# Attention's scan on TensorE: stationary operands of 64 tokens, two in the array, in place of halves of 32 tokens

## The reference, cut to what matters

```
scores  = einsum('bcihn,bcjhn->bcijh', Cc, Bc) * Lm * dtc      # inside a chunk, causal
y_intra = einsum('bcijh,bcjhp->bcihp', scores, xc)
y_cross = einsum('bcthn,bchnp,bcth->bcthp', Cc, h_states, exp(dAcs))
y = y_intra + y_cross + xp * D_param
```

## Time and profile before

| | |
|---|---|
| Time, median of 3 runs | 2917.99 us (2916.21 to 2919.55) |
| Profiled execution, its own time | 2926.86 us |
| Its span | 2925.1 us |
| TensorE matmul, busy | 2769.8 us, 95% of the span |
| TensorE weight load, busy | 2237.4 us, 76% |
| VectorE, busy | 2053.4 us, 70% |
| ScalarE, busy | 1715.0 us, 59% |
| GpSimd, busy | 1463.4 us, 50% |
| Mean granted clock | 0.988 |
| Scan matmuls (L1105) | 16384 records, 169.3 us busy |

### The profile page before, as it was taken

The page is one execution under the profiler, slowest core; times in us unless marked ns, Lnnn a source line. Parts: engine busy times, 40 slices in busy tenths (PEclk is TensorE's granted clock), DMA queues, the critical chain, the costliest instruction groups (busy, mean ns, idle before and its releaser), DMA issues.

```text
span 2925.1 us, 135112 instructions
## 1 busy us (share of the span) xinstructions
PE 2769.8 (95%) x59836; PEld 2237.4 (76%) x59836; DVE 2053.4 (70%) x2871; ACT 1715.0 (59%) x3424; POOL 1463.4 (50%) x2319
## 2 busy tenths in 40 slices
PE   8999999999999999999999999999677787899998
PEld 7888888888888888888888888887566676455554
DVE  6777777777777777777777777777444443788998
ACT  5666566566666666656656656665333333666674
POOL 4666666666667667666666666666110000111111
PEclk9999999999999999999999999999899998899999
DMA  4222222222222222222222222222644443578776
GB/s 154 78 73 69 74 78 76 73 78 77 72 79 74 72 82 73 73 77 74 75 75 78 74 72 79 76 73 58 215 132 136 110 123 119 178 222 269 234 228 195
DMA packets 262711, 316.37 MB, mean 108 GB/s; under 512 B 28000, under 2 KB 184032, under 8 KB 260464
## 3 DMA queue, kind: packets, MB, share of 16 engines
q1 hardware_dynamic: 252176, 297.55, 33.7%
q10 hardware_dynamic: 9952, 10.17, 1.1%
HBM read 194.31 MB, written 113.31 MB: 105 GB/s over the span
## 4 chain that ended last, share of the span: by engine, by line
PE 89%; DVE 4%; issue 4%; DMA 1%; SPq 1%; POOL 1%; ACT 0%; ACTq 0%; DVEq 0%; POOLq 0%
PE a_proj L991 41%; PE a_mix L991 12%; PE s_ps L1714 6%; PE g_pick_ps L1465 6%; PE a_scan L1105 5%; PE s_ps L1735 4%; DVE g_picked L1394 3%; PE s_ps L1730 3%; PE a_scan L1082 3%; PE a_scan L1069 2%; PE g_acc_ps L1489 2%; PE a_mix L1057 2%; PE a_misc L1049 1%; PE a_misc L1123 1%; DMA part_dram<-res 1%
## 5 line engine op out<-in xcount | busy, mean ns | idle before, releaser
L991 PE MATMUL a_proj<-wdh,xTh 128*128 128x512 f32 x1024 | 421.2, 411 | 5.5 <-issue 3.7
L991 PE MATMUL a_proj<-wdh,xTl 128*128 128x512 f32 x1024 | 402.4, 393 | 0.3 <-issue 0.3
L991 PE MATMUL a_proj<-wdl,xTh 128*128 128x512 f32 x1024 | 400.0, 391 | 1.7 <-issue 1.7
L823 DVE COPY_PREDICATED scan_in<-mask,a_scan 64x512 f32<-64x512 uint32 x512 | 382.4, 747 | 16.1
L1671 ACT COPY s_stage<-s_ps 128x1024 f32<-128x1024 f32 x256 | 279.2, 1147 | 150.9 <-PE s_ps L1714 142.4
L464 POOL TENSOR_TENSOR dx<-xs,d_row 64x512 f32<-64x512 f32 x256 | 331.4, 1294 | 15.1
L472 POOL TENSOR_TENSOR yv<-yt,dx 128x512 f32<-128x512 f32 x128 | 189.0, 1476 | 293.2 <-DVE yt L863 293.2
L639 ACT ACTIVATE scan_in<-CT,hsel 64x128 f32<-64x128 f32 x1024 | 326.2, 388 | 4.8
L603 ACT ACTIVATE raw<-a_proj,rs 128x272 f32<-128x272 f32 x128 | 62.5, 488 | 427.4 <-PE a_proj L991 427.4
L1394 DVE COPY g_picked<-g_pick_ps 128x1024 f32<-128x1024 f32 x128 | 156.7, 1224 | 218.4 <-PE g_pick_ps L1465 218.4
L1691 DVE STREAM_TRANSPOSE s_turned<-s_stage 128x2048 f32<-128x2048 f32 x128 | 294.4, 2302 | 9.8 <-ACT s_stage L1671 9.8
(11 more groups left out here) (152 smaller groups left out, 7275.3 us busy)
## 6 DMA issues: line engine op xcount, KB each, us to landing
x<-in_x_dram SPq DMA_DIRECT2D x128, 256.0 KB, 2.7
xn_dram<-xn SPq DMA_DIRECT2D x128, 256.0 KB, 2.4
part_dram<-res SPq DMA_DIRECT2D x128, 256.0 KB, 2.5
g_xn<-xn_dram SPq DMA_DIRECT2D x512, 64.0 KB, 2.3
s_part<-part_dram SPq DMA_DIRECT2D x128, 256.0 KB, 4.1
out_dram<-s_out SPq DMA_DIRECT2D x128, 256.0 KB, 3.8
xr<-in_xT_dram SPq DMA_DIRECT2D x126, 256.0 KB, 2.9
s_inner<-inner_dram SPq DMA_DIRECT2D x32, 512.0 KB, 4.1
```

Of the source, the lines that this page charges most:

```text
L823: nc.vector.copy_predicated(dst, mask[rows_, :].unsqueeze(1).unsqueeze(1).to_broadcast([CH, 4, 2, CH]), src).then_inc(mt_cp, 1)
L991: last = nc.tensor.matmul(out, lhs[a], rhs[c], start=(k == 0 and n == 0), stop=(k == nk - 1 and n == 2))
```

## The change

For each head and chunk the loop over two halves of 32 tokens is gone. The stationary operand is the whole slice of 64 tokens, and the output goes to 64 PSUM partitions at once: chunk 0 uses the array's columns 0 to 63, chunk 1 columns 64 to 127. Per scan there are 32 program matmuls where there were 64. The moving operand, the contraction over 128 rows, the outputs, all semaphores and all other functions are the same.

```diff
             for h in range(H):
                 for c in range(2):
-                    for i in range(0, CH, 32):
-                        out = scan_bank[CH * c + i:CH * c + i + 32, 2 + h // 8, HALF + h % 8 * HD:HALF + (h % 8 + 1) * HD]
-                        last = nc.tensor.matmul(out, scan_in[c][:, h, i:i + 32], xs[c][n % 4][:, h, :], start=True, stop=True)
+                    out = scan_bank[CH * c:CH * c + CH, 2 + h // 8, HALF + h % 8 * HD:HALF + (h % 8 + 1) * HD]
+                    last = nc.tensor.matmul(out, scan_in[c][:, h, :], xs[c][n % 4][:, h, :], start=True, stop=True)
                     if h == H - 1:
                         last.then_inc(y_ps, 1)
```

## The result

The changed kernel takes 2996.3 us (median of 4 runs, 2992.0 to 3003.3) against 2917.6 us: ratio 1.0272, 95% interval 1.0248 to 1.0295. In a later and longer comparison it was 3001.0 against 2920.7, ratio 1.0281 (1.0257 to 1.0304). So it is 79 to 80 us slower by the medians; 100 were forecast, 3018 us, and the range was 2963 to 3048.

The account below looks back on a forecast made before the run. The prediction took TensorE to bound the attention phase, with a column group's turns of weight loads setting the scan's time. Scans +96, tiling +8 and issue -4 made +100 us on 2918: 3018 us, range 2963 to 3048.

Parts of the forecast that it names:

- The number of turns: In a scan each column group keeps 32 loads and matmuls in a row; a 64-column turn takes 58 ns.
- 53 ns: Alternative time of a scan's 64-column load, columns divided by 1.2; the sum would be 3000 us instead of 3018.
- The change of tiling: Ahead of each superstep's first scan TensorE now runs empty when the tile shape changes: 0.12 us, 64 times, +8 us.
- (a): Scan loads stretch from 1.08 to 1.80 us and the last matmul waits 0.03 longer: +0.75 us x 128, +96 us.
- (b): Tile shape now changes ahead of each superstep's first scan: 0.12 us, 64 times, +8 us, bounds 0 and 13.
- term (c): TensorE's issue stalls before scans, 7.7 us, go wholly, in part or move to projections: -4 us, bounds 0 and -8.
- The last rival of the forecast: TensorE's granted clock is halved for as long as the slower scans take: 3248 us, chance 1%.
- term (d): Behind the scan, DVE's L863 hardly moves (0 to 0.1 us) and the chain back to TensorE gains slack: 0.
- Instructions set the pace: Rival: scan records 8.5 ns apart set its time, so half as many make it faster: 2853 us, chance 5%.
- Half of a turn is a fixed hand-over: Rival: a 64-column scan turn takes 46 ns, 12 less than forecast: 2970 us, chance 8%.

Follow-up runs that it names:

- moving8: Changed kernel with 8 of the 32 moving columns in each scan matmul: 3004.5 us, ratio 1.0286 to the kernel before.
- load48: Changed kernel with 48 of the 64 tokens in each scan load, the last 16 of each chunk left out: 2953.6 us in one run.
- gains_moved: Kernel before with spread_gains (L1123) moved from between scores and project_c to right behind the first scan: 2950.7 us against 2919.8, ratio 1.0096.
- after_gains_moved: Changed kernel with spread_gains moved right behind the first scan: 3005.6 us, ratio 1.0291 to the kernel before.
- first_halves: Changed kernel with the old halves of 32 in each superstep's first scan, whole chunks in the second: 2965.8 us, ratio 1.0163 to the kernel before.
- moving64_halves: Kernel before with 64 moving columns in each scan matmul, two heads' x in place of one: 2992.8 us, ratio 1.0258.

## Why the prediction was right in its sign and some 20 us too high

**The number of turns.** Right: 32 per group before and after, loads of 64 columns at 58 ns. That the load and not the moving side sets it is shown by moving8 (no change) and load48 (45 ns). The scan is 0.76 us longer; +0.75 was forecast. (With the 53 ns that it also mentions, the forecast's sum gives 2998 and not 3000.)

**The change of tiling**, 0.12 us ahead of each first scan: as forecast. With the scans it makes 32.98 - 31.38 = 1.60 us per superstep, 64 x 1.60 = +102 us; terms (a) and (b) said +104. That it goes with the change of shape is shown by gains_moved, whose superstep lost 0.12 us with one change less, and by after_gains_moved, where the change of shape stayed and so did the length.

**Issue**, term (c): the step that failed. It was put at -4 us with bounds 0 and -8, from the 7.7 us of waits before scans. By the length of the supersteps, the second to the 62nd, it is -17:

| Kernel | Usual superstep, us | Longer in all, us | Waits called issue, us |
|---|---|---|---|
| before, three traces | 31.38, 31.39, 31.39 | 17.1, 16.9, 16.2 | 13.4, 13.0, 12.3 |
| changed, three traces | 32.98 each | 0 | 0 |
| first_halves | 32.14 | 18.0 | 12.9 |
| moving64_halves | 32.74 | 7.0 | 5.1 |
| gains_moved | 31.27 | 56.0 | 42.8 |

I had not counted the stalls in projections, which come from the same want: the scan had used up the supply in front of them. And I took the waits view for the whole price, which leaves out what lies under the modelled ends of matmuls and the stretch at the lower clock behind one of the stalls. The last rival of the forecast took the clock of 1.00 over the phase to mean that it never falls; it does for a few us in each trace of the kernel before, in the stalls' wake. 13 us of the miss are this term.

**The sum.** +102 - 17 = +85 us. The phase up to the last scan's last matmul grew from 2061.2, 2063.3 and 2059.0 us to 2143.7, 2147.4 and 2144.5, 84 us on average. The missing 1 us lies before the first scan and in the last superstep, which differ by up to 3 us between traces of one kernel.

**The rest of the span**, which the change doesn't touch: 863.9, 864.2 and 855.7 us in three traces of the old scan, 846.5, 854.4 and 855.9 of the new one. The kinds overlap and one kernel differs from itself by 8 us; over all the other variants it goes from 843.3 to 859.7. So the attention phase grew by 84 us in the profiled executions and the medians by 79 to 80; whether the few us between them are a real gain in the rest or chance stays open. The forecast went by the difference of the phase alone.

**Behind the scan**, term (d): DVE's L863 starts at 1013.92 and has waited 0.17 us for the scan, as the timeline shows; before it had no wait.

```profile
1012.82 0.93 DVE L853 TENSOR_TENSOR xs<-gs,decay 64x512 f32<-64x512 f32 x1
1013.92 0.75 DVE L863 SCALAR_TENSOR_TENSOR yt<-a_scan,rs,e 128x512 f32<-128x512 f32 x1 [0.17 <-PE a_scan L1104]
```

Nobody on TensorE waits for it, so it costs nothing, as forecast.

**The rivals.** "Instructions set the pace" had a true core: instructions do limit, but as rare stalls, 17 us in all, not in each turn. "Half of a turn is a fixed hand-over" (46 ns) was built on three gaps in a group of 16 columns; 45 ns is what 48 columns take, 64 take 58, and the fixed part is some 6 ns.

## What to carry to other kernels

When small matmuls lie side by side in column groups, count the turns of one group and multiply by the longer of its load and its moving part; the number of instructions is not the cost. A wider stationary operand in fewer groups gives each group as many turns, each of them longer, and may add a change of tiling. The order matters as well: neighbours must lie in different groups. Before putting small matmuls together to save such a change, look at how many instructions already run at full pace ahead of them. And take the price of stalls from the length of whole supersteps: here the view of waits showed 13 us where 17 were lost.

## What the runs showed of the hardware

A turn of a column group took 45 and 58 ns for loads of 48 and 64 columns, which is 0.81 ns per column and some 6 ns fixed. With 32 columns it was 34 ns with four groups in turn and 29 ns in one group alone. With 32 stationary and 64 moving columns it was 55 ns.

TensorE can outrun its supply of instructions. A first scan of 256 instructions in 1.2 us costs 17 us in the whole kernel, 320 in 1.5 us cost 56, and 256 in 1.9 us still 7, by the length of the supersteps. 128 in 1.6 to 2.0 us, and 256 in 3.9, cost none. The stalls are up to 2.5 us long and in the kernel before they repeat two supersteps apart. All of them end 1.2 to 1.6 us after a block of 256 instructions has landed. Why only a superstep's first scan is hit is open.
